# Output weights loaded and summed earlier, their signs on ScalarE alone, sparse activations masked in place, second step and last steps reordered

## The reference, cut to what matters

```python
xn = _layernorm(x)
x = x + attention(xn) + ffn(xn)
# attention: q, k, v = xn @ Wq, Wk, Wv; rotary on q and k; 16 heads of 32
#   per chunk of 128 rows, kv is the state carried from chunk to chunk:
#   inter = (q * q_decay) @ kv;  intra = ((q @ k.T) * dmask) @ v
#   kv = r_C * kv + (k * k_decay).T @ v;  out = rms_norm(inter + intra) @ Wo
# ffn: W_syn is 2048 x 512, W_out is 512 x 2048, both ternary
#   scale = mean(|W|); q = clip(round(W / (scale + 1e-8)), -1, 1) * scale
z = xn @ ternary(W_syn).T + b_syn
thresh = the 204th largest value of each row of z
hidden = where(z >= thresh, relu(z), 0)
out = layernorm(xn + hidden @ ternary(W_out).T + b_out, gamma, beta)
```

## Time and profile before

| | |
|---|---|
| median of 3 runs | 987.25 us (987.02 to 987.45) |
| the profiled execution | 984.96 us |
| its span | 983.0 us |
| PE busy | 931.6 us, 95% of the span |
| DVE busy | 847.4 us, 86% |
| POOL busy | 755.6 us, 77% |
| ACT busy | 586.7 us, 60% |

### The profile page before, as it was taken

One profiled execution on the slowest core, in us unless ns is written; L12 is line 12 of the kernel. 1 busy time (PEld: TensorE's weight loads), 2 busy tenths in 40 slices (PEclk: granted clock), 3 DMA queues, 4 the chain that ended last, 5 costly groups with the idle time before them and its releaser, 6 DMA issues.

```text
span 983.0 us, 19271 instructions
## 1 busy us (share of the span) xinstructions
PE 931.6 (95%) x6771; PEld 486.2 (49%) x6771; DVE 847.4 (86%) x2294; ACT 586.7 (60%) x777; POOL 755.6 (77%) x653
## 2 busy tenths in 40 slices
PE   5856999999999999999999999999999999999986
PEld 2423455555555555554555555545555555455542
DVE  6889989888898898888988888888898888888876
ACT  7869456666555566665555666655566665555651
POOL 2844688887888888889888888898888888988642
PEclk9978999999999999999999999999999999999988
DMA  9866644554564456556444654565546547544450
GB/s 327 217 235 128 119 87 87 119 107 99 118 108 98 89 95 119 98 107 119 99 96 90 105 118 91 115 119 98 91 83 118 112 93 119 108 104 80 77 97 32
DMA packets 322371, 111.08 MB, mean 113 GB/s; under 512 B 308448, under 2 KB 308704, under 8 KB 321504
## 3 DMA queue, kind: packets, MB, share of 16 engines
q1 hardware_dynamic: 318432, 102.42, 53.0%
q10 hardware_dynamic: 3840, 7.41, 2.1%
HBM read 24.34 MB, written 8.39 MB: 33 GB/s over the span
## 4 chain that ended last, share of the span: by engine, by line
PE 85%; DVE 5%; DMA 4%; POOL 3%; issue 2%; SPq 1%; ACT 1%; ACTq 0%; DVEq 0%; POOLq 0%
PE proj L890 44%; PE p_ffn L1000 11%; PE p_ffn L1006 10%; PE p_wo L1018 8%; PE p_av L962 3%; PE sbank L953 3%; PE p_av L973 3%; DMA area<-in_L_ffn_W_syn_dram 1%; PE sbank L898 1%; DMA area<-in_L_attn_Wk_dram 1%; PE sbank L1059 1%; DVE xrn L1328 1%; DMA area<-in_L_attn_Wo_dram 1%; POOL area L676 1%; DMA area<-hl 0%
## 5 line engine op out<-in xcount | busy, mean ns | idle before, releaser
L890 PE MATMUL proj<-wqkv,xT 128*128 128x512 f16 x1152 | 259.7, 382 | 2.3 <-DVE area L1267 2.2
L890 PE MATMUL proj<-wsynT,xT 128*128 128x512 f16 x1024 | 240.6, 383 | 0.0
L890 PEld LDWEIGHTS proj<-wqkv,xT 128*128 128x128 f16 x1152 | 111.9, 99 | 129.6 <-issue 6.9
L890 PEld LDWEIGHTS proj<-wsynT,xT 128*128 128x128 f16 x1024 | 95.6, 98 | 101.7 <-issue 3.3
L717 POOL TENSOR_TENSOR hl<-area,hl 128x2048 f16<-128x2048 f32 x31 | 126.5, 4081 | 2.3 <-ACT hl L534 2.3
L1000 PE MATMUL p_ffn<-woutT,area 128*128 128x512 f16 x496 | 118.9, 383 | 2.0 <-DMA area<-hl 2.0
L1006 PE MATMUL p_ffn<-woutT,area 128*128 128x512 f16 x496 | 112.1, 379 | 0.0
L448 ACT ACTIVATE area<-area 128x1024 f16<-128x1024 f32 x64 | 64.1, 1049 | 78.8 <-POOL area L671 78.8
L1374 DVE MAX8 cand<-area 128x8 f32<-128x128 f32 x512 | 107.9, 278 | 1.1
L722 POOL TENSOR_TENSOR ahl<-pair_a,ahl 128x512 f16<-128x512 f32 x32 | 37.1, 1158 | 91.4 <-DVE area L1474 88.8
L1474 DVE SCALAR_TENSOR_TENSOR area<-area,c 128x2048 f32<-128x2048 f32 x32 | 75.2, 2352 | 26.7 <-POOL hl L717 26.6
(11 more groups left out here) (232 smaller groups left out, 1817.4 us busy)
## 6 DMA issues: line engine op xcount, KB each, us to landing
xrn<-in_L_attn_x_dram SPq DMA_DIRECT2D x32, 256.0 KB, 3.1
out_dram<-pair_b SPq DMA_DIRECT2D x32, 256.0 KB, 2.1
woutT<-in_L_ffn_W_syn_dram ACTq DMA_DIRECT2D x2, 1024.0 KB, 10.9
area<-in_L_ffn_W_syn_dram ACTq DMA_DIRECT2D x2, 1024.0 KB, 11.9
woutT<-in_L_ffn_W_out_dram SPq DMA_DIRECT2D x2, 1024.0 KB, 11.4
area<-in_L_attn_Wq_dram ACTq DMA_DIRECT2D x1, 1024.0 KB, 7.2
area<-in_L_attn_Wk_dram ACTq DMA_DIRECT2D x1, 1024.0 KB, 9.5
area<-in_L_attn_Wv_dram ACTq DMA_DIRECT2D x1, 1024.0 KB, 11.7
```

The source lines that it names most:

```text
L890: last = nc.tensor.matmul(bank, xT[:, b.par, k, :], w, start=m == 0, stop=m == len(pairs) - 1)
```

## The change

1. **Loading and sums.** The four quarters of W_out are loaded from ScalarE's queue: quarter 1 behind the last load of W_syn, quarters 2 and 3 after the first two sign passes of W_syn, quarter 0 before `syn_flat(3)`. ScalarE sums quarter 1 before `syn_flat(3)` and the others after `wo_rows`, all ahead of step 0. PE spreads the sum behind `projection(1, 3)`. The mean is made by one small ScalarE instruction (`out_mean`), the thresholds by two on POOL.
2. **Signs.** Quarter 3 also goes through ScalarE. Order of the quarters: 2, 3, 0, 1 instead of 3, 2, 1, 0. Quarter 1, both passes, and its addition now lie in step 1: on ScalarE behind `qkv_out(b, 2)`, on DVE behind `attention_added` and `segments(t, 3)`.
3. **Masking in place.** `hidden` writes into z; `below` no longer waits for `lo_ready`, and `z_chunk(b, 0)` waits for it instead (same half of z).
4. **Steps 0 and 1.** The two early projections of tile 2 move back into step 1, `z_chunk(1, 3)` too. In step 1 SP transposes quarters 0 and 1 ahead of `high_transposed(0)`; `second_count` on ScalarE comes before `hidden_high`.
5. **Last steps.** `squares_summed(T31)` goes into the middle of `network_high(T30)`, `failures` and `factors_spread` of T31 into the middle of `network_low(T30)`, the first z transposes of T31 between matmuls 8 and 9 of `attention_projected(T31)`. On DVE `selection(T31)` starts before `mean_square(T31)`, which is put inside it.

The diff, cut to what the prediction speaks of:

```diff
# SP
             def step(sp, i, p):
+                if u and u.n == 0:
+                    out_transpose(0)
+                    sp.wait_ge(S["outT0"], 16)
+                    load_x(4)
+                    out_transpose(1)
                 if u:
                     high_transposed(u)
-                    if u.n == 0:
-                        out_transpose(0)
...
                 if b and b.n == 1:
-                    sp.wait_ge(S["out_sign"], 2)
+                    sp.wait_ge(S["out_sign"], 5)
+                    out_transpose(2)
                     out_transpose(3)
-                    out_transpose(2)
-                    out_transpose(1)
                     sp.wait_ge(S["outT2"], 16)
                     load_x(3)
# ScalarE
+            def out_mean():
+                act.wait_ge(S["out_sum"], 1)
+                nc.scalar.activation(pc[:, 8:12], rowsums["out"], ACT.Copy, scale=1.0 / (N * E),
+                                     accum_out=scale_out).then_inc(S["out_mean"], 1)
...
                 sign("syn", syn_in[1], syn_other[1], syn_thr[1])
                 sign("syn", syn_in[1], syn_t[1], syn_thr[0])
+                act.wait_ge(S["syn_tern"], 1)
+                load_out(2)
+                act.wait_ge(S["syn_sign"], 2)
+                load_out(3)
...
+                act.wait_ge(S["synT0"], 16)
+                act.wait_ge(S["syn_flip"], 4)
+                load_out(0)
+                sums("out", (1,))
                 syn_flat(3)
                 heads_state(first)
                 wo_rows()
+                sums("out", (2, 3, 0))
...
+            def second_step():
+                a, b, t, u = Tile(1, 1), Tile(1, 0), Tile(0, 1), Tile(0, 0)
+                heads_state(t)
+                diagonal(u)
+                first_count(t)
+                act.wait_ge(S["outT3"], 16)
+                sign("out", out_in[0], out_t[0], out_thr[0])
+                qkv_out(b, 0)
+                second_count(t)
+                hidden_high(u, z[:, u.par, :])
+                attention_high(u)
+                qkv_out(b, 1)
+                third_count(t)
+                qkv_out(b, 2)
+                act.wait_ge(S["out_tern0"], 1)
+                sign("out", out_in[1], signs_b, out_thr[1])
+                sign("out", out_in[1], out_t[1], out_thr[0])
+                normalised(a)
# PE, step
-                    for n in range(2 if b.n == 2 else 0, 3):
+                    for n in range(3):
...
                 projection(b, 3)
+                if t.n == 0:
+                    sums_spread("out")
...
-                if t.n == 0:
-                    sums_spread("out")
                 projection(b, 5)
                 projection(b, 6)
-                if t.n == 0:
-                    projection(Tile(1, 0), 0)
-                    projection(Tile(1, 0), 1)
# PE, last steps
-                network_high(T30)
-                squares_summed(T31)
-                network_low(T30)
-                wait(pe, "att_added", T31, 1, 0)
-                factors_spread(T31)
-                last_failures()
-                attention_projected(T31)
-
-                last_flipped(0)
+                network_high(T30, lambda: squares_summed(T31))
+                network_low(T30, last_sums)
+                attention_projected(T31, lambda: last_flipped(0))
+
# VectorE
                 if n == 0:
-                    wait(dve, "h_ready", b, 1, -1)
+                    wait(dve, "lo_ready", b, 1, -1)
...
             def below(t):
                 wait(dve, "nt_step", t, 5, 5)
-                wait(dve, "lo_ready", t, 1, -1 if t.n == NT - 1 else 0)
...
+            def following_step():
+                t, b, a, u = Tile(0, 1), Tile(1, 0), Tile(1, 1), Tile(0, 0)
+                search_begun(t)
+                first_step(t)
+                q_decayed(t)
+                row_stats(a)
+                attention_normalised(u)
+                row_shift(a)
+                ternary_of_signs(0, 7)
+                second_step(t)
+                below(t)
+                segments(t, 0)
+                segments(t, 1)
+                segments(t, 2)
+                probs(t, 0)
+                probs(t, 1)
+                z_chunk(b, 0)
+                probs(t, 2)
+                probs(t, 3)
+                z_chunk(b, 1)
+                attention_added(u)
+                segments(t, 3)
+                dve.wait_ge(S["out_mean"], 1)
...
+                ternary_of_signs(1, 9)
+                selection(t)
+                z_chunk(b, 2)
...
                 segments(T31, 2)
-                mean_square(T31)
                 segments(T31, 3)
+                selection(T31, lambda: mean_square(T31))
                 factors(T31)
-                selection(T31)
```

More of the change, by code:

```diff
@@ L478, in prologue @@
                 load_syn(3)
+                load_out(1)
                 qkv_sums(2)
@@ L1015, in attention_projected @@
                 for m, (l, w, g) in enumerate(terms):
+                    if l and g == 0 and between:
+                        between()
                     if l and g == 0:
```

260 lines of the change are left out of this document (145 added, 115 removed).

## The result

The changed kernel takes 990.36 us, the median of 10 runs (989.12 to 993.38), against 987.13 for the kernel before, measured beside it: a ratio of 1.0043, 95% interval 1.0027 to 1.0059. It is slower, by 2.7 to 5.8 us. The forecast was no change, 987.1, with 983.0 to 990.5 as its range; the case that came is rival B. The profiled execution took 989.12 us with a span of 987.1, that is 4.1 more than the span before.

The account below looks back on a forecast made before the run. PE's work was taken to bound the middle, so only start and end could move: start +2.3, half clock +1.8, end -4.3, sum -0.2, giving 987.1 us, with a range of 983.0 to 990.5.

Parts of the forecast that it names:

- rival B: Prologue: ScalarE waits for W_syn's quarter 0 transpose, slowed by loads of W_out; 990.1 us with 3 us delay; chance 0.16.
- (a): Prologue: two DMA issues and the sum of quarter 1 on ScalarE make `wo_rows` end 1.1 us later.
- (g): Start of `network_high(0)`: after PE idles 7 us, the first 8 or so matmuls run at half clock, +1.8 us.
- the end: PE's last blocks: `attention_projected(T31)` starts 2.4 us earlier, without a gap, at full clock; -4.3 us in all.
- (b): Step 0 on DVE: 5.85 us of mean, thresholds and quarter 3 goes, quarter 1's addition moves; `mean_square(0)` at 82.3.
- (c) to (f): Step 1, chain over ScalarE, POOL, PE, DVE and SP: `network_high(0)` starts at 115.0, 2.3 us later than before.
- The middle: Between 112 and 930 us: masking in z gains 0, since PE is busy throughout.
- The sum: Whole kernel: 2.3 + 1.8 - 4.3 = -0.2, that is 987.1 us; chance 0.50.

Follow-up runs that it names:

- the kernel with the masking apart: The changed kernel with the masked activations in their own buffer again, `below` waiting for `hidden_low`: 997.21 us against 985.69 for the kernel before.
- the first trace: Profiled execution of the changed kernel's first measurement, span 987.1; the second is of the same kernel measured again unaltered, span 991.3, median 993.05 us.
- the kernel with last steps and masking: The kernel before with the new last steps and the masked activations kept in z, no more: 981.69 us against 984.27, ratio 0.9968.
- the last steps alone: The kernel before with only the last-steps part of the change: 983.12 us against 985.69, ratio 0.998.

## Why the prediction was wrong

**(a) the prologue is the step that failed.** It priced ScalarE's two DMA issues and one more pass, +1.1. No run has just these with transposes that land in 4.4 us, so the 1.1 itself is not tested. But it took no cost for what the issued transfers do to others. The wait for the transpose of quarter 0 came to 5.29 us, `row_flipped(4)` was +5.9, PE then ran 8 matmuls at half clock, and `first_count(0)` was +7.5. The prediction had this as rival B, with the place, the queue behind it and the point of 2.2 us from which it decides, at 0.16; its argument against it, that over 8 us of ScalarE's work cover the landing, took 4.2 to 5.3 us from the earlier trace rows, rows of transposes with hardly a plain load beside them. Those rows bound the landing from below only, and the trace of before had no row for the other end. The 8 us were too many as well: ScalarE was through with that work at 41.99, 7.7 us after the transpose was issued. B's time of 990.1 is close to the 990.36 measured partly by luck: it was worked out for a delay of 3 us, the mark came 5.7 later than forecast, and (g) and the end each gave back 0.7.

**(b) step 0** held: from `first_count(0)` to `mean_square(0)` 23.8 instead of 30.7 us, 6.9 saved, 6.2 predicted. **(c) to (f)** held to 0.1 us as a whole: from `mean_square(0)` to the mark 32.7 was predicted and 32.64 measured, its links within 0.4 (`hidden_high(0)` done 10.4 behind `mean_square(0)` and not 10.6, `attention_low(0)` 16.8 and not 17.1, quarter 1's addition 23.8 and not 24.0). The mark itself was predicted at 115.0 and came at 120.70: the difference is the 6.4 by which (a) was short, less the 0.7 that (b) gained. (A slip in the prediction: without the shared port `hidden_low(0)` would start 1.1 earlier by its own numbers, 93.0 instead of 94.1, and not 1.3.) **(g)** +1.8 was a little high: PE idled 7.87, the first 8 matmuls took 3.32, 1.4 more, and T30 lost 1.1.

**The middle, 0:** held, PE is busy for 800.00 of 800.00 us. `below` has a mean of 2.91 us instead of the 3.2 expected, so its wait and its length together fell from 75.2 + 26.7 to 93.2 + 1.1 us, and nobody gained by it. Step 1 alone is different, as the kernel with the masking apart shows: there the predicted chain holds only because `below(1)` needn't wait.

**The end, -4.3:** right in mechanism, 5.0 in the first trace and 3.3 in the second. **The sum** with (a) as measured is 7.5 - 6.9 + 7.4 + 1.1 - 5.0 = +4.1; 7.4 is what steps 0 and 1 as reordered cost behind `mean_square(0)` (32.6 against 25.3). The kernel with quarter 1 ahead of quarter 0 takes 4.7 of it away; the other 2.7 stay there although PE comes to the mark without a wait, and step 1 holds 24 matmuls more than before.

What stays open: the runs give the last steps 0.3 to 3.6 us where traces give 3.2 to 5.3, and the changed kernel 3.2 us of loss at one time and 8.8 at another. Part of it is the scatter of the prologue and of the clock at the end, shown above; how often each happens no trace tells, nor what makes the prologue begin late.

## What to carry to other kernels

When loads move to another queue, look up which transposes or waits are in flight at the new time: the rows of a transfer that runs alone are the lower bound of its landing, not its price. A slow landing costs only what waits for it: with the same two loads the old order had no engine waiting and no loss that can be told, the new one had `first_count(0)` 4.8 us later than with the loads moved behind, and loads moved behind two transposes slowed the next two. And when a wait at one place is taken out, read what stands behind it on each queue before pricing the gain: here the gain moved from one wait to the next until the loads and two orders had been changed together, for 9.9 us. Last, compare a place in a trace with traces of kernels that leave it alone, before calling 3 us an effect.

## What the runs showed of the hardware

**A DMA transpose slows to a third beside plain loads from the other queue.** The DMA queues' own record, of the kernel before, where only three loads of 0.26 MB from its own queue follow the transpose (34 to 39 us), and of the changed kernel beside two loads (34 to 47 us); q1 is SP's queue, q10 ScalarE's:

```profile
q1 hardware_dynamic: 2187, 0.73, 67.9%
```
```profile
q10 hardware_dynamic: 288, 2.10, 50.9%
q1 hardware_dynamic: 2323, 0.96, 50.7%
```

Some 2,100 packets of under 512 bytes (of the 2,323) share the engines with 288 packets that hold 2.10 MB. The transpose landed after 4.4 us without a load of 1 MB, 7.6 with one beside it, 10.6 to 12.5 with two. Its issue on SP grew too, from 1.94 to 5.80 us, and what stands behind it on SP came later. The Trainium skill ("DMA: Bandwidth & Descriptors", section "Queues, rings and completion order") says that each DMA engine takes turns between the queues it has work for, a whole packet at a time, and in "Issuing engines are not separate DMA queues" that all of them run on the same 16 engines. That fits these rows; no run here varied the size of a packet, so the mechanism is not shown.

**The port shared by DVE and POOL.** `hidden_low(0)` took 5.12 us where it crossed `below(1)`, 4.08 where it didn't (the kernel with the masking apart). In the kernel with last steps and masking DVE's 128x2048 addition began 0.5 after `hidden_low(0)` and took 4.63, and `hidden_low(0)` 4.06; with the last steps alone it began 0.5 ahead and took 1.22, and `hidden_low(0)` 4.67. The Trainium skill ("SBUF — State Buffer", "Who interferes with whom") has it as an exclusive lock; by these rows either engine can be the one that is held.
